# Edge sort: ScalarE sets the index columns of 27 instead of 22 blocks before its wait for the u-term; LN3: a group's statistics stand before the rows of the group before it

## The reference, cut to what matters

```python
# first graph step: the mean of the edge attributes by source node, then an MLP over [LN(x), mean, u]
sums = segment_sum(edge_attr, src); counts = segment_sum(ones, src)
combined = concatenate([LN(x), sums / maximum(counts, 1), u[batch]])       # batch is 0 everywhere
x = x + relu(combined @ W1 + b1) @ W2 + b2
x = x + dense_ffn(LN(x))                                                   # top 2 of 8 experts, one choice for all
# second graph step: h = LN(x) @ W, gathered by src, scaled by the degrees, summed by dst
x = x + segment_sum(h[src] * norm, dst)
# second FFN: each token of LN(x) goes to its best expert of 8, at most 977 tokens each
x = x + y_ffn
```

## Time and profile before

| what | us |
|---|---|
| median of 3 runs | 3339.6 |
| lowest and highest | 3337.01, 3344.58 |
| the profiled execution, its own time | 3332.7 |
| its span | 3330.8 |

### The profile page before, as it was taken

One profiled execution on the slowest core, in us unless ns is written; L12 is line 12 of the kernel. 1 busy time (PEld: TensorE's weight loads), 2 busy tenths in 40 slices (PEclk: granted clock), 3 DMA queues, 4 the chain that ended last, 5 costly groups with the idle time before them and its releaser, 6 DMA issues.

```text
span 3330.8 us, 49254 instructions
## 1 busy us (share of the span) xinstructions
PE 2283.8 (69%) x14349; PEld 2086.2 (63%) x14350; DVE 2011.2 (60%) x3304; ACT 884.0 (27%) x2321; POOL 2033.4 (61%) x1707
## 2 busy tenths in 40 slices
PE   0000188369899475997877882778887876598997
PEld 0000177268888475775877771667676665598997
DVE  8789899023333131465566665875665554489887
ACT  0000033100000000133444431334444412254553
POOL 5778377777777774011444433667777731288886
PEclk9999999655555555798999996989988975599999
DMA  6542155365444252121011113557777733322231
GB/s 203 149 113 72 51 158 165 110 167 128 112 117 115 64 135 69 51 75 50 29 39 44 46 47 107 156 159 194 190 194 192 199 87 111 85 62 66 76 85 35
DMA packets 341516, 358.58 MB, mean 108 GB/s; under 512 B 209280, under 2 KB 248560, under 8 KB 341125
## 3 DMA queue, kind: packets, MB, share of 16 engines
q1 hardware_dynamic: 209538, 196.84, 20.2%
q0 software_dynamic: 105984, 93.52, 12.3%
q10 hardware_dynamic: 25853, 66.46, 6.4%
HBM read 234.90 MB, written 122.85 MB: 107 GB/s over the span
## 4 chain that ended last, share of the span: by engine, by line
POOL 29%; PE 21%; DVE 19%; issue 17%; DMA 8%; DVEq 3%; ACT 2%; POOLq 0%; SPq 0%; ACTq 0%
POOL sorted L996 21%; POOL mid L1073 5%; DMA x_rows<-mid 3%; PE ps L2039 3%; PE ps L2139 2%; DVE ps L1217 2%; POOL h_lo L1035 2%; DVE big L1244 2%; PE ps L1990 2%; DVE yb L1880 2%; DVEq L1605 2%; PE ps L2094 2%; PE ps L2017 2%; PE ps L2096 1%; PE ps L2095 1%
## 5 line engine op out<-in xcount | busy, mean ns | idle before, releaser
L1990 PE MATMUL ps<-big 128*128 128x65 f32 x2380 | 528.0, 419 | 206.2 <-DVE big L1371 156.9
L1990 PEld LDWEIGHTS ps<-big 128*128 128x128 f32 x2380 | 514.0, 331 | 221.4 <-issue 220.2
L1073 POOL DMA_INDIRECT mid<-h_rows,idx_a x400 | 484.3, 1211 | 177.7 <-issue 113.3
L1370 DVE COPY mid<-big 128x28 f32 (+1 forms) x85 | 20.4, 240 | 568.8 <-PE ps L1990 354.0
L1005 POOL TENSOR_TENSOR rstd<-var,neg_half 125x2 f32<-125x2 f32 (+1 forms) x100 | 69.6, 696 | 456.2 <-DVE var L1422 456.2
L996 POOL DMA_INDIRECT sorted<-xh,idx_b x200 | 237.3, 1187 | 114.1 <-issue 60.6
L996 POOL DMA_INDIRECT sorted<-yb,idx_a x200 | 237.6, 1188 | 83.9 <-issue 60.0
L996 POOL DMA_INDIRECT sorted<-mid,idx_b x200 | 237.4, 1187 | 66.3 <-issue 66.0
L996 POOL DMA_INDIRECT sorted<-wk,idx_a x200 | 237.3, 1186 | 61.0 <-issue 60.7
L1615 DVE TENSOR_TENSOR hT<-ps,mid 128x608 bf16<-128x608 f32 (+3 forms) x245 | 255.1, 1041 | 0.1
L2139 PE MATMUL ps<-mid 125*128 125x96 f32 x1600 | 224.4, 304 | 38.1 <-issue 15.4
(11 more groups left out here) (331 smaller groups left out, 6485.2 us busy)
## 6 DMA issues: line engine op xcount, KB each, us to landing
h_in_r<-h_parts SPq DMA_DIRECT2D x245, 256.0 KB, 4.2
big<-sorted ACTq DMA_DIRECT2D x85, 469.0 KB, 4.8
sorted<-hT SPq DMA_DIRECT2D x73, 469.0 KB, 7.5
mid<-in_L_ffn_w SPq DMA_DIRECT2D x16, 1024.0 KB
hid_x<-hT ACTq DMA_DIRECT2D x25, 500.0 KB
mid<-hid_x SPq DMA_DIRECT2D x25, 500.0 KB, 3.3
h_parts<-h_part_r SPq DMA_DIRECT2D x25, 500.0 KB
mid<-h_rows,idx_a POOLq DMA_INDIRECT x400
```

What stands on the lines that cost most here:

```text
L1073: nc.gpsimd.indirect_dma_start(mg4[:, s, i, :], None, h_rows, bass.IndirectOffsetOnAxis(idx4[:, s, i:i + 1], 0)).then_inc(s_gk[s], 16)
L1990: i_ = mm(banks[:, bass.ds(o_, CW)], node_hot[:, s % 2, i, :], rows2[:, s, i, 0:CW], start=False, stop=True, skip_group_check=True)
```

## The change

A constant moves five blocks' columns (22 to 26) in ACT's list from the loop over the groups to ahead of the wait for the u-term. In the loop the same places now hold blocks 27 to 42, and the first loads of sorted rows follow block 43's columns instead of block 42's. In LN3's body on DVE, the wait for `s_x3c`, the statistics of group g and the logits of group g-3 now stand ahead of the normalised rows of group g-1. No instruction is added or removed.

```diff
-XH_AT = 22
+XH_AT = 27
...
             def gate_group(g, s=None):
                 fixed = isinstance(g, int)
                 s = g % 2 if s is None else s
+                if not (fixed and g < 2):
+                    dve.wait_ge(s_x3c, g - 1)
+                settle()
+                ln_stats(lambda t: x[:, bass.ds(g * GT + t, 1), :].rearrange("p a d -> p (a d)"), s, stat, mv, var, s_v3,
+                         None if fixed and g < 3 else lambda: logits(g - 3, 1 - s))
                 if not (fixed and g == 0):
                     ln3_rows(g - 1, 1 - s)
-                if not (fixed and g < 2):
-                    dve.wait_ge(s_x3c, g - 1)
-                settle()
-                ln_stats(lambda t: x[:, bass.ds(g * GT + t, 1), :].rearrange("p a d -> p (a d)"), s, stat, mv, var, s_v3,
-                         None if fixed and g < 3 else lambda: logits(g - 3, 1 - s))
```

More of the change, by code:

```diff
@@ L1728, in gate_group @@
                 s = g % 2 if s is None else s
-                if not (fixed and g == 0):
-                    ln3_rows(g - 1, 1 - s)
                 if not (fixed and g < 2):
@@ L1735, in gate_group @@
                          None if fixed and g < 3 else lambda: logits(g - 3, 1 - s))
+                if not (fixed and g == 0):
+                    ln3_rows(g - 1, 1 - s)
             in_turns(dve, st, gate_group, G, 4, 3, 2)
```

## The result

The changed kernel takes 3329.84 us (median of 15 runs, 3325.38 to 3339.18), the kernel before 3340.39 (15 runs, 3333.01 to 3344.58). The ratio is 0.9972, with a 95% interval of 0.9963 to 0.9981: 9.4 us less, from 6.3 to 12.4. The prediction was 3326.8 and a gain of 12.8. (The gain is taken from the ratio; the two medians themselves are 10.6 apart.)

What follows compares the result with a forecast made beforehand. POOL's puts into `sorted` were taken to bound the edge sort, stores to bound LN3. 7.2 + 5.3 + 0.3 = 12.8 us off the median of 3339.6 gave 3326.8 us, range 3318 to 3336.

Steps and rivals of the forecast that it cites:

- What held POOL, and what holds it next: Ahead of block 22: POOL's 53.4 us wait ends at ACT's columns; after the change, block rows landing at 409.7 end it.
- twice the lag: Block 22's rows: if their semaphore lags twice as much as the weights' did, first put at 411.5, 6.3 us gained.
- The 12.5 us of the sort: Edge sort, POOL's puts: 7.2 us gained ahead of block 22 and 5.3 ahead of block 23, bounds 11.6 and 13.2.
- ACT's new wait and the late groups: ACT in the edge sort: block 26's columns wait for block 22's put, delaying bias and 25 groups, without cost.
- The reserve: Edge sort: block 61's columns come 14 us before POOL needs them, against 20 us at block 60 before.
- the rival of the starved POOL: Edge sort near block 61: 0.3 us more per group uses up 14 us; at 0.6 more, 3340 us; chance 0.04.
- The clock in the 25 groups: Rival: PE stays at the lower clock in the edge sort's groups, POOL loses 17 us, 3344 us; chance 0.03.
- the new loop: LN3: rows, transposes, gate products, logits and statistics close in 4.1 us a group, under the stores' 4.69, costing nothing.
- The 0.1 for two semaphores: LN3: allowance of 0.1 us for two semaphores within the 4.1 us a group.
- the 0.3 us of gain at the start: LN3's first seven microseconds: group 1's store to `out` comes 1.5 us earlier, gaining 0.3 us, upper bound 1.3.
- the bound of 0.8: LN3's start: a loss of 0.8 us if ACT's second stage copy waits out all of group 0's delayed rows.
- the three rivals that it calls 0.17 together: Starved POOL, 3340 us, chance 0.04; LN3's loop longer than its stores, 3341.4, 0.05; LN3 faster, 3309, 0.04.

Runs made afterwards that it cites:

- The two repeats: The kernel before run again, 3336.4 us (one run), and the changed kernel run again, 3324.05 us, ratio 0.9962 to before.
- Two blocks' columns: Columns of only blocks 22 and 23 moved, LN3 old, against the kernel before: 3321.72 us, ratio 0.9957; again 3324.11 us, 0.9957.
- the runs one part at a time: Against the kernel before: five blocks' columns alone, 3325.12 us, ratio 0.9970; LN3's new order alone, 3337.13 us, ratio 0.9999.
- the rows early: Rows of blocks 22 to 25 issued ahead of SP's wait: changed kernel 0.9834, same with LN3 old 0.9826, kernel before 1.0005.

## Why the prediction was right, point by point

**What held POOL, and what holds it next.** The prediction let the columns go 100 us early and the rows be late next, with a hole of 45 to 47 us ended by the landing of the rows. It is 47.44 us, ended by `in_edge_attr`. The time from issue to first put, worked out from packets and a lag, was 9.6 us, and measured 9.36. The first put itself was 1.1 us later than predicted, because SP's issue was 1.35 later in that execution. One of the prediction's bounds is slightly off: with twice the lag its own numbers give 409.0 + 1.4 + 0.87 = 411.3 and not 411.5, so that the lower bound of the sort is 11.8; nothing rests on it.

**The 12.5 us of the sort.** 7.2 for block 22 and 5.3 for block 23 were predicted. From SP's first weight load to the last put it is 888.1 us in the profile of before and 875.6 in that of the changed kernel: 12.5. The two repeats, both with puts of 1190 ns, have 889.4 and 877.8: 11.6. Two blocks' columns give all of it (875.3 and 875.7 in their two profiles).

**ACT's new wait and the late groups.** Predicted: bias at 427.8, ACT's group work ends at 675.7, the first sum at 689.1; measured: 431.37, 676.75, 689.43. The bias is 3.6 us late: block 22's last put was issued at 425.24, 1.2 later than predicted, and block 26's columns start 5.8 us behind it, where the prediction took the median landing of 3.8; the bias stands behind these columns. The groups behind it wait for later puts, so that only 1 us of this reaches their end. The reserve was misread. The prediction has 14 us at block 61, counted from the last of 46 loads; 45 stand ahead of that block, and the smallest reserve measured is 20.3 us, at block 60, as before the change. The price of the rival of the starved POOL (0.3 us more a group uses it up) is therefore too high: with 20 us it takes 0.44. No wait of POOL for ACT came, so this rival fell; the kernel with two blocks, whose groups are not late, starts its next stage at the same time.

**The clock in the 25 groups.** Busy PE by stretch in the changed kernel (us, PE busy, granted clock, DMA share, GB/s):

```profile
455.00:500.00 45.00, 32.93 (x234) 0.81 0.47 133
...
460.00:463.00 3.00, 3.00 (x10) 0.50 0.43 93
...
500.00:640.00 140.00, 106.44 (x761) 0.79 0.50 147
```

The clock falls to 0.50, 1.2 GHz, at the start of a burst, as in the earlier trace rows, and comes back inside it: the mean is 0.79 to 0.81. Between 455 and 640 us ACT waited 71.7 us in all for puts ahead of its columns, and POOL took each block's columns 42.4 us or more after they were set. That rival fell. What the Trainium skill describes (TensorE: Matmul & The Clock Gate, HAM oscillation), bursts that start at the low clock behind a wait, is seen here: eight products take 3.70 us behind waits of 5.60 and 4.61 us (459.38 and 474.38), and 1.96 us at 489.62, behind one of 1.44. It costs nothing here, since ACT still reaches each block's columns ahead of the put that it needs.

**LN3.** That stores bind it, and that the new loop closes under them, held: 4.1 us predicted, 3.95 in the mean and 4.23 in the round shown, against 4.69 for the stores. (The 0.1 for two semaphores came from no row; in the round shown it is 0.2 from the end of the products to the logits.) The term that was mis-sized is the 0.3 us of gain at the start: measured is a loss of 0.7 us, and of 1.1 against the commoner value of the old order, at or just beyond the bound of 0.8. The cause given for the gain was that group 1's store to `out` starts earlier and fills a bubble. It does start earlier: 0.34 us behind the first store of the stage instead of 1.47. But the rate of the first stretch did not rise, and the first store of the stage took 6.87 us to land instead of the 5.92 of before:

```profile
2729.08 5.92 DMA x_rows<-mid
```

The same is seen in all profiles with full stores: 6.79 to 6.87 us in the four with the new order, 5.32 to 6.03 in the seven with the old one. So most of the 1.1 us arises at this store, which ACT waits for before it fills the same buffer again. That the earlier bytes slow it by sharing the DMA engines is the likely reason, and was not tried by itself.

**The total.** 12.8 us were predicted; the ratio says 9.4 (6.3 to 12.4), the repeat of the full change 0.0038 x 3336.3 = 12.7, and the two runs of two blocks 14.3 each. The predicted 12.8 lies just above the first interval and inside that of the repeat. The puts kept 11.6 to 12.5 us in the pairs of profiles that are alike but for the change; a loss behind them of a few us is neither shown nor excluded, as the graph step scatters by more. That the repeat came within 0.1 us of 12.8 is partly luck: its interval goes from 8 to 17 us, the sort gave 12.3 instead of 12.5 in the runs one part at a time, and LN3's 0.3 has the wrong sign. The prediction's own bounds also add up a little wider than it says: 11.6 - 0.8 = 10.8 is 2.0 below 12.8, not 1.7, and the three rivals that it calls 0.17 together have 0.13.

## What to carry to other kernels

When a wait is to be removed, read when each of the instruction's other inputs is there, from issue to landing: the gain reaches only to the next of them, and moving that one alone gave nothing (ratio 1.0005). A hole with two releasers needs both edits, and the second can be a constant in another engine's list. Where a reserve is claimed, find the instruction that it belongs to by its buffer and its count in the list: one load more or less ahead of a block is 7 us here. Where a stage is bound by stores, a longer loop of engines is free only up to their interval, and must be read with the stores taken away to know how near it is.

## What the runs showed of the hardware

- An indirect put of 125 rows took 1187 ns in the median in nine profiles and 1190 in four (the repeats of before and of the full change, and the first two with the rows early). Over 800 puts that is 2.4 us without any change in the kernel: with the rows early, the last put came at 1231.9 in one such execution and at 1229.5 in one with 1187 (LN3's order differs between the two, long behind the puts). With the rows early, single puts between 393 and 412 us took up to 2.00 us, in part beside block rows and weight loads.
- SP's first weight load was issued between 398.4 and 401.8 us in 13 profiles, and the graph step took 654.8 to 670.8 us. Times counted inside one profile from an event that the change doesn't touch agree much better than totals: from that load to the last put it is 887.6 to 888.1 us in three profiles with 22 blocks ahead and 875.3 to 875.9 in five with 24 or 27, all with puts of 1187 ns.
- Cutting LN3's store to `out` to 5 of 125 partitions left 94 GB/s of traffic in the old order, against 114 with full stores: near half of the bytes of a group were gone, and the time from the first to the last store fell from 109.4 (110.8 in the first profile) to 68.8 us.

```profile
2754.00:2782.00 28.00, 25.06 (x117) 24.13 (x118) 18.65 (x79) 13.56 (x40) 6.56 (x10) 0.50 0.32 94
```

In this stretch of that kernel PE is busy for 25.06 of 28 us at the lower clock, against 17.6 in the earlier trace rows: LN3 without most of its stores stands close to what PE can do at 1.2 GHz.
